# A projection weight read in quarters: its first piece in two halves, a small matrix requested later, and the first batch's input transposed at later steps

## The chip, the cores and the metric

The kernel runs on one NeuronCore of one Trainium2 chip. The metric is device time in microseconds (us): the median of several executions, each measured from start to end on the device. The engines of the core are TensorE (PE, matrix products; PEld is its weight load), VectorE (DVE), ScalarE (ACT), GpSimd (POOL) and SyncE (SP). SP and ACT also issue the DMA requests here; their queues are SPq and ACTq.

## The reference

Shapes: x is 8 batches of 512 tokens by 2048. A is 8 adapters of 2048x16 and B is 8 adapters of 16x2048 (the "cond" weights); W (`base_w`) is 2048x2048; `ffn_A` is 64x2048, `ffn_B` is 16 experts of 2048x64, `router_w` is 16x2048. Everything is float32.

```
cond    = (x @ B[id].T) @ A[id].T                     # rank 16, one adapter id for each batch
base    = cond @ W.T + base_b
hidden  = cond @ ffn_A.T                              # 64 wide
probs   = softmax(cond @ router_w.T)                  # 16 experts
combine = one_hot(top2(probs)) * (top2 / sum of top2)
delta   = sum over experts e of combine[e] * (hidden @ ffn_B[e].T)
out     = x + base + 0.5 * delta
```

## The kernel before, in words

Because cond has rank 16, the kernel never forms `cond @ W.T` for the tokens. It first builds G = W A for all 8 adapters (a 128x2048 matrix, 8 batches x 16 ranks by outputs). Then each batch needs only bx = B x (16 ranks by 512 tokens, spread over the partitions), the router on bx, and tile products of 128 tokens by 512 outputs.

**The setup stage** (up to the first tile of batch 0) reads W in 8 pieces of 256 rows (2 MB each, `load_w`, four requests of 512 KB, two from SP and two from ACT). The four buffers of `w_in` take turns. A piece gives 16 steps, so there are 128 steps `n` = 0 to 127: piece `g = n // 16`, slice `s = n % 16` of the contraction. In step n VectorE transposes a strided 128x256 slice of W into one of 8 places of a ring (`w_transpose(n)`, line 659, counted on semaphore `w_transposed`), and TensorE multiplies it with the gathered A (`w_product(n)`, line 866, two matmul rows in the trace for each product, counted on `w_used`). VectorE may be at most 8 steps ahead of TensorE, since `w_transpose(n)` waits until product n-8 is done.

Everything else of the setup is woven between these steps by tables of step numbers, written out by hand. All engines walk the same n, each at its own pace, and each executes its own list strictly in order:

- `BT_AT`: VectorE transposes B (`b_transposes`, line 665) after that step. `FA_AT`: it transposes ffn_A and router_w (line 647). `GLO_AT` = 40: at steps 40, 72 and 104 it splits a finished part of G (`take_g`, lines 695 and 701).
- `X_AT`: at which step VectorE transposes the j-th pair of slices of batch 0's x (line 728, from the buffer `xquad0`, four requests of 1 MB, line 290, two from each queue). There are 16 pairs. The tables `BX_AFTER` tell TensorE after which step it does the 16 products of the first and of the second half of x (line 941).
- `E_AT`: before which step TensorE flips expert group g (`expert_flips`, line 856, 8 transposes; written here as flips(g)). It waits for the group's load, `e_in`, written here as e0 to e15, requested by `load_experts` (line 250; steps in `E_LOAD_AT` on ACT, program order on SP). ACT copies the flipped group out (`copy_experts`, line 495, two activations 64x1024).
- `SLOT_AT`: the router chain of batch 0 in slots. Slot 8: ACT copies the finished bx products out of PSUM (`bxp`, the row `tmp<-ps`). Slot 9: TensorE forms the logits (line 949) and spreads bx (line 952), VectorE takes the row maximum (line 751) and subtracts it, ACT takes the exponential (line 554) and copies bx. Slot 10: VectorE finds the top two (lines 756 to 772). Slot 11: VectorE builds the combine matrix (lines 776 to 788). On VectorE a slot comes `SLOT_LAG` = 4 steps later than its table entry, on TensorE and ACT right at it. Inside one step n ACT runs its expert copy (`E_AT`) before its slot (`SLOT_AT`); TensorE runs the flips, the product, and then the slot.

The requests of SP and ACT go out in program order too. On ACT: token ids, A, W pieces 0 and 1, B, piece 2, the small matrices, e0, piece 3, e1, piece 4, e2, piece 5, e3, e4, x of batch 0, e5, piece 6, e6, e7, piece 7. SP's list is alike, with a small request for the bias rows (line 362) behind e1; e4 on both queues waits until these rows have landed (`s_biasrow`).

**The batch stage** then runs 8 batches of 16 tiles. Each tile is seven matmuls of 128x128 by 128x512 (lines 927 to 930), and one VectorE addition into the resident x (line 840).

Of the kernel before, what the change touches and what calls it, by code (L numbers as in the profile page):

```python
# [37 lines left out]
RING = 8  # L38
# [3 lines left out]
def adaln_ffn(nc, x, itok, cond_A, cond_B, base_w, base_b, ffn_A, ffn_B, router_w, out):  # L42
# [5 lines left out]
    KD = D // P  # L48
# [32 lines left out]
    with ExitStack() as ctx:  # L81
# [81 lines left out]
        s_load = [[sem(f"w_loaded{k}_half{h}") for k in range(WB)] for h in range(2)]  # L163
        s_ein = [sem(f"expert_in{k}") for k in range(7)]
# [44 lines left out]
        X_AT = {82 + 3 * j // 2: j for j in range(KD)}  # L209
        BX_AFTER = {90: 3, 101: 8}  # L210
        SLOT_AT = {103: 8, 106: 9, 109: 10, 112: 11, 115: 12, 119: 13, 123: 14}
        SLOT_LAG = 4
        GA_AFTER, SEL_AFTER = 42, 62
        BT_AT, FA_AT, GA_AT, SEL_AT = 24, 36, 56, 72
# [9 lines left out]
        WIDE_FROM = 2 * NT  # L224

# [65 lines left out]

        def load_w(eng, n, qs):

            need(eng, s_wt, (n - WB + 1) * KD)
            for q in qs:
                eng.dma_start(w_in[n % WB][q * SQ:(q + 1) * SQ], w_q[n, q]).then_inc(s_load[q // 2][n % WB], 16)  # L296
# [34 lines left out]
        def _(sp):  # L331
# [17 lines left out]
            load_w(sp, 0, (0, 1))  # L349
            sp.dma_start(bias_n[:, 0, :], base_b.rearrange("(a o) -> a o", a=BR)).then_inc(s_bias, 16)  # L350
            load_w(sp, 1, (0, 1))
            load_cond_b(sp, (0, 1))
# [4 lines left out]
            load_w(sp, 3, (0, 1))  # L357
            load_experts(sp, 1, 0)
# [134 lines left out]
        def _(act):  # L493
# [5 lines left out]
            load_w(act, 0, (2, 3))  # L499
            load_w(act, 1, (2, 3))  # L500
            load_cond_b(act, (2, 3))
# [4 lines left out]
            load_w(act, 3, (2, 3))  # L506
            load_experts(act, 1, 1)
# [5 lines left out]
            def copy_experts(g):  # L513

                act.wait_ge(s_ef, g + 1)
                for at, there, count in ((0, s_a, NB), (0, s_bT, KC), (1, s_fat, 2), (1, s_sm, 1),
                                         (2, s_xe, 2 * KD)):
                    if g == PER_C * at:
                        act.wait_ge(there, count)
                c, q, i = e_where(g)  # L520
                src = ps[:, e_bank(g):e_bank(g) + 2, :].rearrange("p b o -> p (b o)")\
                    .rearrange("p (a h m) -> p a m h", a=EG, h=2)
                dst = bexpT[q * R:(q + 1) * R, c, i * EG:(i + 1) * EG, :].rearrange("r a (m h l) -> r l a m h", h=2, l=2)
                for l in range(2):
                    ins = copy(dst[:, l], src[l * R:(l + 1) * R])
                ins.then_inc(s_ec, 1)
# [90 lines left out]
        def _(dve):  # L617
# [31 lines left out]
            def w_transpose(n):  # L649

                g, s = n // KD, n % KD
                if s == 0:
                    for half in range(2):
                        dve.wait_ge(s_load[half][g % WB], (g // WB + 1) * NQ // 2 * 16)
                need(dve, s_wmm, n - RING + 1)
                if n == 0:
                    dve.wait_ge(s_const, 1)
                src = w_in[g % WB].rearrange("p t (l r) -> p r t l", l=SQ)[:, s]
                dve.transpose(wT[:, n % RING, :].rearrange("p (t l) -> p t l", l=SQ), src).then_inc(s_wt, 1)  # L659

# [136 lines left out]
            take_a()  # L797
            for n in range(NW):
# [52 lines left out]
        def _(pe):  # L851
# [6 lines left out]
            def w_product(n):  # L858

                g, s = n // KD, n % KD  # L860
                if n == 0:
                    pe.wait_ge(s_a, NB)
                if s == 0:
                    need(pe, s_glo, g // 2 - 1)
                pe.wait_ge(s_wt, n + 1)
                pe.matmul(ps[:, ACC + g // 2 % 2, g % 2 * WN:(g % 2 + 1) * WN], a_t[:, s, :], wT[:, n % RING, :],  # L866
                          start=(s == 0), stop=(s == KD - 1)).then_inc(s_wmm, 1)

# [97 lines left out]
            first = Batch(0)  # L966
            for n in range(NW):
# [50 lines left out]
```

## Time and profile before

| | us |
|---|---|
| median of 3 runs | 446.18 |
| lowest, highest | 445.64, 464.56 |
| the profiled execution, whole | 445.62 |
| its span, first to last instruction | 443.8 |
| mean granted TensorE clock | 0.996 of full |

The profiled execution is the reference for all sums: its span is 443.8 us and 1.8 us lie around the span. Its whole time is 0.02 us under the lowest of the three runs; the highest run, 464.56 us, is far from the other two. The setup stage ends when the first tile's matmuls begin, 116.3 us after the span's start; the rest are the 8 batches.

### The profile page before, as it was taken

The page shows a single profiled execution, that of the slowest core. Times are in us where ns is not written, and L with a number is a line of the kernel's source. Part 1 is how long each engine was busy: PE and PEld are TensorE (multiplying, and loading weights), DVE is VectorE, ACT ScalarE, POOL GpSimd, SP SyncE. Part 2 cuts the span into 40 slices and gives each one's busy share as a digit, 9 for nine tenths or more (in the row PEclk, how much of TensorE's full clock was granted, in tenths as well). Part 3 has the DMA queues.
Part 4 walks back from the last instruction along what each step waited for, and adds up shares of the span by engine and source line. Part 5 has one row for each costly group of instructions (what it writes and reads, how often), then busy time and mean ns, then how long its engine had stood idle before and what let it go on. Part 6 is the DMA issues. An engine that isn't in the chain of part 4 may idle for free.

```text
span 443.8 us, 6785 instructions
## 1 busy us (share of the span) xinstructions
PE 409.7 (92%) x2496; PEld 279.9 (63%) x2496; DVE 319.4 (72%) x830; ACT 108.1 (24%) x163; POOL 40.5 (9%) x53
## 2 busy tenths in 40 slices
PE   0597997999788999999999999999999999999996
PEld 0475985656556766666667666666666676666665
DVE  2699996999468496668677875966686778756453
ACT  0003114435473231123113112311231131123110
POOL 4020000002100120012001201200120012012000
PEclk9999998999999999999999999999999999999999
DMA  8999999999999999899999999998999898556935
GB/s 223 357 330 331 334 357 366 345 269 336 289 295 239 352 362 323 279 349 342 310 287 378 306 315 302 366 312 295 348 335 325 285 366 303 207 201 217 343 128 189
DMA packets 75027, 135.35 MB, mean 305 GB/s; under 512 B 5506, under 2 KB 14770, under 8 KB 74994
## 3 DMA queue, kind: packets, MB, share of 16 engines
q1 hardware_dynamic: 56000, 102.08, 69.7%
q10 hardware_dynamic: 18994, 32.84, 23.5%
q8 instruction: 20, 0.33, 0.3%
q14 instruction: 13, 0.11, 0.1%
HBM read 99.23 MB, written 35.65 MB: 304 GB/s over the span
## 4 chain that ended last, share of the span: by engine, by line
PE 63%; DVE 10%; DMA 9%; SPq 6%; POOL 3%; ACT 3%; issue 3%; ACTq 2%; POOLq 0%; DVEq 0%
PE ps L927 13%; PE ps L928 11%; PE ps L929 11%; PE ps L901 11%; PE ps L941 6%; DMA bexpT<-in_x 6%; PE ps L930 5%; POOL u_r L480 3%; DMA gm_r<-xT 3%; DVE xT L728 3%; DVE early L659 3%; SPq L296 3%; ACT bexpT L495 2%; PE ps L856 2%; PE ps L949 2%
## 5 line engine op out<-in xcount | busy, mean ns | idle before, releaser
L840 DVE TENSOR_TENSOR xbuf<-ps,xbuf 128x512 f32<-128x512 f32 x128 | 86.7, 677 | 96.0 <-PE ps L930 96.0
L927 PE MATMUL ps<-h_r,u_r 128*128 128x512 f32 x256 | 108.8, 425 | 0.7
L928 PE MATMUL ps<-h_r,u_r 128*128 128x512 f32 x256 | 100.3, 392 | 0.0
L929 PE MATMUL ps<-h_r,u_r 128*128 128x512 f32 x256 | 100.1, 391 | 0.0
L866 PE MATMUL ps<-early 128*128 128x256 f32 x256 | 66.5, 408 | 22.6 <-DVE early L659 22.6
L728 DVE STREAM_TRANSPOSE xT<-xbuf 128x256 f32<-128x256 f32 x224 | 80.6, 410 | 0.0
L866 PEld LDWEIGHTS ps<-early 128*128 128x128 f32 x256 | 48.1, 201 | 36.8 <-issue 16.5
L927 PEld LDWEIGHTS ps<-h_r,u_r 128*128 128x128 f32 x256 | 48.1, 188 | 35.9 <-issue 16.7
L659 DVE STREAM_TRANSPOSE early<-xbuf 128x256 f32<-128x256 f32 x128 | 65.9, 577 | 5.3 <-issue 3.8
L901 PE MATMUL ps<-bexpT,cur 128*32 128x512 f32 x512 | 61.6, 598 | 2.2 <-DVE h_r L707 1.5
L495 ACT ACTIVATE h_r<-ps 128x512 fp32r<-128x512 f32 x64 | 36.2, 595 | 78.8 <-PE ps L901 78.4
L929 PEld LDWEIGHTS ps<-h_r,u_r 128*128 128x128 f32 x256 | 48.1, 188 | 10.9
L928 PEld LDWEIGHTS ps<-h_r,u_r 128*128 128x128 f32 x256 | 48.2, 188 | 9.8 <-issue 1.7
L930 PE MATMUL ps<-gm_r,sbx_r 128*128 128x512 f32 x128 | 50.1, 391 | 0.0
L495 ACT ACTIVATE bexpT<-ps 64x1024 f32<-64x1024 f32 x32 | 35.2, 1101 | 50.6 <-issue 21.5
L707 DVE TENSOR_TENSOR h_r<-ps,h_r 128x512 fp32r<-128x512 f32 x64 | 40.4, 671 | 3.7 <-ACT h_r L495 3.7
L901 PEld LDWEIGHTS ps<-bexpT,cur 128*32 128x32 f32 x512 | 13.5, 109 | 32.5 <-issue 30.3
L941 PE MATMUL ps<-xT,bT 128*32 128x256 f32 x512 | 33.3, 381 | 0.2 <-DVE xT L728 0.2
L473 POOL TENSOR_TENSOR sbx_r<-bx,sbx_r 32x512 fp32r<-32x512 f32 x8 | 10.4, 1297 | 241.2 <-ACT sbx_r L495 241.2
L941 PEld LDWEIGHTS ps<-xT,bT 128*32 128x32 f32 x512 | 17.3, 109 | 17.0 <-issue 5.1
L480 POOL TENSOR_TENSOR u_r<-tmp,u_r 128x512 fp32r<-128x512 f32 x16 | 20.6, 1287 | 74.1 <-ACT u_r L495 74.0
L930 PEld LDWEIGHTS ps<-gm_r,sbx_r 128*128 128x128 f32 x128 | 24.0, 188 | 5.2
(67 smaller groups left out, 205.3 us busy)
## 6 DMA issues: line engine op xcount, KB each, us to landing
out<-xbuf SPq DMA_DIRECT2D x31, 1024.0 KB, 7.3
xbuf<-in_x SPq DMA_DIRECT2D x28, 1024.0 KB, 7.4
xbuf<-in_x ACTq DMA_DIRECT2D x32, 512.0 KB, 10.9
xbuf<-in_x SPq DMA_DIRECT2D x32, 512.0 KB, 8.6
xbuf<-in_L_ffn_base_w SPq DMA_DIRECT2D x16, 512.0 KB, 19.3
xbuf<-in_L_ffn_base_w ACTq DMA_DIRECT2D x16, 512.0 KB, 20.1
gm_r<-g_hilo SPq DMA_DIRECT2D x128, 32.0 KB, 6.8
early_u<-in_L_ffn_B SPq DMA_DIRECT2D x10, 256.0 KB, 18.5
```

Source lines behind the costliest of these rows:

```text
L495: return act.activation(dst, src, ACT.Copy)
L659: dve.transpose(wT[:, n % RING, :].rearrange("p (t l) -> p t l", l=SQ), src).then_inc(s_wt, 1)
L707: dve.tensor_tensor(h_r[:, c % 2, 1, h, :], ps[:, HB + h, :], f32(h_r[:, c % 2, 0, h, :]), ALU.subtract).then_inc(s_hlo, 1)
L728: dve.transpose(xh[:, place, :].rearrange("p (t l) -> p t l", l=SQ), src).then_inc(s_xe, 1)
L840: dve.tensor_tensor(xs, ps[:, tile_bank(b.n, m), :], xs, ALU.add).then_inc(s_out, 1)
L866: pe.matmul(ps[:, ACC + g // 2 % 2, g % 2 * WN:(g % 2 + 1) * WN], a_t[:, s, :], wT[:, n % RING, :], start=(s == 0), stop=(s == KD - 1)).th ...
L901: ins = pe.matmul(ps[32 * j:32 * j + 32, HB + h, :], cur[:, b.q, 0:2 * RK], bexpT[:, c, 4 * h + j, :], start=True, stop=True)
L927: pe.matmul(acc, u_r[:, b.q, 0, h, tok_t], hi, start=(h == 0), stop=False)
L928: pe.matmul(acc, u_r[:, b.q, 0, h, tok_t], lo, start=False, stop=False)
L929: pe.matmul(acc, u_r[:, b.q, 1, h, tok_t], hi, start=False, stop=False)
L930: pe.matmul(acc, sbx_r[:, b.q, tok_t], gm_r[:, c * BANK:(c + 1) * BANK], start=False, stop=True)\
L941: pe.matmul(ps[at:at + BK, BXB, g * (T // 2):(g + 1) * (T // 2)], bT[:, j, f.half, :], xh[:, ring_place(f, j), :], start=(j < NQ), stop=(j ...
```

## The change

W's first piece is requested in two halves of 128 rows (each quarter request of 512 KB becomes two of 256 KB; the two first halves of each queue go out ahead of the second ones), with semaphores of its own. VectorE and TensorE go through the 16 slices with the first half (`first_transpose`, `first_product`, 128 wide), then again with the second half (the new branch for `n < KD` in `w_transpose` and `w_product`), and from step 16 on as before. B is requested behind W's piece 3 in place of behind piece 1, on both queues, and transposed after step 46 in place of 24. ffn_A goes from step 36 to 34. The 16 pairs of batch 0's x go from steps 82, 83, 85, ... 104 to steps 88, 89, 90, 91, 93, ... 106. `BX_AFTER` and `SLOT_AT` follow.

```diff
-        X_AT = {82 + 3 * j // 2: j for j in range(KD)}
-        BX_AFTER = {90: 3, 101: 8}
-        SLOT_AT = {103: 8, 106: 9, 109: 10, 112: 11, 115: 12, 119: 13, 123: 14}
+        X_AT = {88 + 5 * j // 4: j for j in range(KD)}
+        BX_AFTER = {94: 3, 104: 8}
+        SLOT_AT = {105: 8, 107: 9, 110: 10, 112: 11, 115: 12, 119: 13, 123: 14}
...
-        BT_AT, FA_AT, GA_AT, SEL_AT = 24, 36, 56, 72
+        BT_AT, FA_AT, GA_AT, SEL_AT = 46, 34, 56, 72
...
+        WT = WN // SQ // 2
...
+        def load_first_w(eng, qs):
+
+            for h in range(2):
+                for q in qs:
+                    eng.dma_start(w_in[0][q * SQ:(q + 1) * SQ, h * WT:(h + 1) * WT], w_q[0, q, :, h * WT:(h + 1) * WT])\
+                       .then_inc(s_w0[q // 2] if h == 0 else s_load[q // 2][0], 16)
...
             load_cond_a(sp, 0)
-            load_w(sp, 0, (0, 1))
+            load_first_w(sp, (0, 1))
             sp.dma_start(bias_n[:, 0, :], base_b.rearrange("(a o) -> a o", a=BR)).then_inc(s_bias, 16)
             load_w(sp, 1, (0, 1))
-            load_cond_b(sp, (0, 1))
             load_w(sp, 2, (0, 1))
             sp.wait_ge(s_const, 1)
             load_small(sp, (0, 1))
             load_experts(sp, 0, 0)
             load_w(sp, 3, (0, 1))
+            load_cond_b(sp, (0, 1))
             load_experts(sp, 1, 0)
...
                 act.wait_ge(s_ef, g + 1)
-                for at, there, count in ((0, s_a, NB), (0, s_bT, KC), (1, s_fat, 2), (1, s_sm, 1),
-                                         (2, s_xe, 2 * KD)):
-                    if g == PER_C * at:
+                for first, there, count in ((0, s_a, NB), (2, s_bT, KC), (PER_C, s_fat, 2), (PER_C, s_sm, 1),
+                                            (2 * PER_C, s_xe, 2 * KD)):
+                    if g == first:
                         act.wait_ge(there, count)
...
                 need(dve, s_wmm, n - RING + 1)
-                if n == 0:
-                    dve.wait_ge(s_const, 1)
+                if n < KD:
+                    wide = wT[:, n % RING, :].rearrange("p (h t l) -> p h t l", h=2, l=SQ)
+                    src = w_in[0][:, WT:2 * WT].rearrange("p t (l r) -> p r t l", l=SQ)[:, s]
+                    dve.transpose(wide[:, 1], src).then_inc(s_wt, 1)
+                    return
...
+            def first_transpose(s):
+
+                if s == 0:
+                    for half in range(2):
+                        dve.wait_ge(s_w0[half], NQ // 2 * 16)
+                    dve.wait_ge(s_const, 1)
+                need(dve, s_wmm0, s - RING + 1)
+                wide = wT[:, s % RING, :].rearrange("p (h t l) -> p h t l", h=2, l=SQ)
+                src = w_in[0][:, 0:WT].rearrange("p t (l r) -> p r t l", l=SQ)[:, s]
+                dve.transpose(wide[:, 0], src).then_inc(s_wt0, 1)
...
+                if n < KD:
+                    pe.wait_ge(s_wt, n + 1)
+                    pe.matmul(ps[:, ACC, WN // 2:WN], a_t[:, s, :], wT[:, n % RING, WN // 2:WN],
+                              start=(s == 0), stop=(s == KD - 1)).then_inc(s_wmm, 1)
+                    return
...
+            def first_product(s):
+
+                if s == 0:
+                    pe.wait_ge(s_a, NB)
+                pe.wait_ge(s_wt0, s + 1)
+                pe.matmul(ps[:, ACC, 0:WN // 2], a_t[:, s, :], wT[:, s % RING, 0:WN // 2],
+                          start=(s == 0), stop=(s == KD - 1)).then_inc(s_wmm0, 1)
```

How the tables move the instructions is seen best in the engines' own lists. The first place is TensorE from the product of step 82 on, where line 866 (895 after) is the W product, line 856 (882) the flips and line 941 (978) the products with x. Before:

```order
L866 MATMUL ps<-early 128x256 x6
L856 MATMUL ps<-ident,early_u 128x128 x8
L866 MATMUL ps<-early 128x256 x3
L941 MATMUL ps<-xT,bT 32x256 x16
L866 MATMUL ps<-early 128x256
L856 MATMUL ps<-ident,early_u 128x128 x8
```

The same place after:

```order
L895 MATMUL ps<-early 128x256 x6
L882 MATMUL ps<-ident,early_u 128x128 x8
L895 MATMUL ps<-early 128x256 x4
L882 MATMUL ps<-ident,early_u 128x128 x8
L895 MATMUL ps<-early 128x256 x3
L978 MATMUL ps<-xT,bT 32x256 x16
```

The flips before steps 88 and 92 keep their steps (they are expert groups 5 and 6); the first 16 products with x went from behind step 90, between the two flips, to behind step 94, after both.

The second place is VectorE from its last transposes of x to the maximum of the router (line 728, after 752: x; 659, after 672: W; 695 and 701, after 719 and 725: `take_g` of step 104; 751, after 775: the maximum in slot 9). Before:

```order
L728 STREAM_TRANSPOSE xT<-bexpT 128x256 x2
L695 CAST u_r<-ps 128x512
L701 TENSOR_TENSOR u_r<-ps,u_r 128x512
L659 STREAM_TRANSPOSE early<-xbuf 128x256 x6
L751 TENSOR_REDUCE mx<-ps 128x4
L753 TENSOR_TENSOR ex<-ps,mx 128x64
```

After:

```order
L719 CAST u_r<-ps 128x512
L725 TENSOR_TENSOR u_r<-ps,u_r 128x512
L672 STREAM_TRANSPOSE early<-xbuf 128x256
L752 STREAM_TRANSPOSE xT<-bexpT 128x256 x2
L672 STREAM_TRANSPOSE early<-xbuf 128x256
L752 STREAM_TRANSPOSE xT<-bexpT 128x256 x2
L672 STREAM_TRANSPOSE early<-xbuf 128x256 x5
L775 TENSOR_REDUCE mx<-ps 128x4
```

The last pair of x now stands behind `take_g`, with five transposes of W between it and the maximum, where `take_g` and six transposes stood.

The third place is ACT from the copy of bx out of PSUM (slot 8) to the copies of bx in slot 9; `bexpT<-ps` x2 is one expert copy. Before:

```order
L495 ACTIVATE tmp<-ps 128x512
L250 DMA bexpT<-in_L_ffn_B 64x4x256
L554 ACTIVATE ex<-ex 128x64
L495 ACTIVATE bx<-ps 128x512
L495 ACTIVATE sbx_r<-bx 64x512
L495 ACTIVATE bexpT<-ps 64x1024 x2
```

After:

```order
L505 ACTIVATE tmp<-ps 128x512
L253 DMA bexpT<-in_L_ffn_B 64x4x256
L505 ACTIVATE bexpT<-ps 64x1024 x2
L564 ACTIVATE ex<-ex 128x64
L505 ACTIVATE bx<-ps 128x512
L505 ACTIVATE sbx_r<-bx 64x512
```

The copy of expert group 8 went from behind slot 9 to ahead of its exponential, because slot 9 moved from step 106 to 107, the step of that copy.

## Rows read from the trace of the kernel before

**Rows 1.** The page, section 2: busy share of the DMA engines in 40 slices of 11.1 us.

```profile
DMA  8999999999999999899999999998999898556935
```

**Rows 2.** Waits of TensorE from 112 us on, the largest: total us, times, longest.

```profile
PE ps L856 <- ACT bexpT L495: 3.0, 4, 0.8
```

**Rows 3.** Timeline of VectorE, first 72 us: start us, us, instruction, count, idle before.

```profile
15.37 12.44 DVE L659 STREAM_TRANSPOSE early<-xbuf 128x256 f32<-128x256 f32 x25 [3.84 <-issue]
...
35.99 2.85 DVE L647 STREAM_TRANSPOSE bexpT<-bexpT 128x768 f32<-128x768 f32 x2
...
47.83 3.10 DVE L659 STREAM_TRANSPOSE early<-xbuf 128x256 f32<-128x256 f32 x6 [0.76 <-PE ps L866]
...
60.29 1.11 DVE L659 STREAM_TRANSPOSE early<-xbuf 128x256 f32<-128x256 f32 x2 [0.71 <-PE ps L866]
...
71.76 0.77 DVE L728 STREAM_TRANSPOSE xT<-bexpT 128x256 f32<-128x256 f32 x2 [3.49 <-DMA bexpT<-in_x]
```

**Rows 4.** ACT's two requests for W's first piece, and their landing.

```profile
L296 ACTq DMA_DIRECT2D xbuf<-in_L_ffn_base_w x2: 601/622/644, 2.0 to 2.7; - x2
DMA to landing us min/median/max: 10.5/11.5/12.6
```

**Rows 5.** The chain that ended last, its longest piece: start us, us, what.

```profile
47.18 24.46 DMA bexpT<-in_x
```

**Rows 6.** Timeline of VectorE, 85 to 98 us.

```profile
85.74 0.73 DVE L728 STREAM_TRANSPOSE xT<-bexpT 128x256 f32<-128x256 f32 x2
86.39 0.57 DVE L659 STREAM_TRANSPOSE early<-xbuf 128x256 f32<-128x256 f32 x1
86.88 0.73 DVE L728 STREAM_TRANSPOSE xT<-bexpT 128x256 f32<-128x256 f32 x2
...
93.11 0.66 DVE L695 CAST u_r<-ps 128x512 fp32r<-128x512 f32 x1
...
94.40 3.08 DVE L659 STREAM_TRANSPOSE early<-xbuf 128x256 f32<-128x256 f32 x6
...
97.54 0.23 DVE L751 TENSOR_REDUCE mx<-ps 128x4 f32<-128x64 f32 x1
```

**Rows 7.** SP's two requests for W's piece 6, and their landing.

```profile
L296 SPq DMA_DIRECT2D xbuf<-in_L_ffn_base_w x2: 2620/2918/3217, 56.9 to 60.2; - x2
DMA to landing us min/median/max: 19.3/19.5/19.7
```

**Rows 8.** SP's request for e5, and its landing.

```profile
L250 SPq DMA_DIRECT2D early_u<-in_L_ffn_B x1: 2247/2247/2247, 54.6 to 54.6; - x1
DMA to landing us min/median/max: 19.1/19.1/19.1
```

**Rows 9.** SP's request for e6, and its landing.

```profile
L250 SPq DMA_DIRECT2D early_u<-in_L_ffn_B x1: 2820/2820/2820, 62.8 to 62.8; - x1
DMA to landing us min/median/max: 18.2/18.2/18.2
```

**Rows 10.** Timeline of TensorE matmuls, 68 to 98 us.

```profile
73.07 3.76 PE L866 MATMUL ps<-early 128*128 128x256 f32 x8 [2.86 <-DVE early L659]
...
80.41 2.29 PE L941 MATMUL ps<-xT,bT 128*32 128x256 f32 x32
...
83.16 1.04 PE L856 MATMUL ps<-ident,early_u 128*128 128x128 f32 x8
84.03 2.75 PE L866 MATMUL ps<-early 128*128 128x256 f32 x12
...
92.92 0.94 PE L941 MATMUL ps<-xT,bT 128*32 128x256 f32 x4 [0.20 <-DVE xT L728]
```

**Rows 11.** Timeline of ACT and its queue, 93 to 101 us.

```profile
93.95 1.74 ACTq L250 DMA_DIRECT2D xT<-in_L_ffn_B  x2
95.78 0.60 ACT L495 ACTIVATE tmp<-ps 128x512 f32<-128x512 f32 x1 [4.93 <-issue]
...
99.66 1.07 ACT L495 ACTIVATE bexpT<-ps 64x1024 f32<-64x1024 f32 x1
```

**Rows 12.** Stretch 74 to 76 us: length, busy PE, PEld, DVE, ACT, POOL, granted clock, DMA share, GB/s.

```profile
74.00:76.00 2.00, 2.00 (x5) 1.32 (x5) 2.00 (x6) 1.31 (x2) 0.00 (x0) 0.50 1.06 366
```

More of the change, by code:

```diff
@@ L163, in adaln_ffn @@
         s_load = [[sem(f"w_loaded{k}_half{h}") for k in range(WB)] for h in range(2)]
+        s_w0 = [sem(f"w_first_half{h}") for h in range(2)]
+        s_wt0, s_wmm0 = sem("w_first_transposed"), sem("w_first_used")
         s_ein = [sem(f"expert_in{k}") for k in range(7)]
@@ L498, in _ @@
             load_cond_a(act, 1)
-            load_w(act, 0, (2, 3))
+            load_first_w(act, (2, 3))
             load_w(act, 1, (2, 3))
-            load_cond_b(act, (2, 3))
             load_w(act, 2, (2, 3))
@@ L506, in _ @@
             load_w(act, 3, (2, 3))
+            load_cond_b(act, (2, 3))
             load_experts(act, 1, 1)
@@ L797, in _ @@
             take_a()
+            for s in range(KD):
+                first_transpose(s)
             for n in range(NW):
@@ L860, in w_product @@
                 g, s = n // KD, n % KD
-                if n == 0:
-                    pe.wait_ge(s_a, NB)
+                if n < KD:
[3 more added lines that the diff above has]
+                    return
                 if s == 0:
@@ L966, in _ @@
             first = Batch(0)
+            for s in range(KD):
+                first_product(s)
             for n in range(NW):
```

## The prediction

> **What bounds the kernel now.** I read three things, in this order. First, from 112 us on TensorE is the engine that the rest wait for: its largest wait of the whole batch stage is 3.0 us in four pieces [rows 2]. So whatever the setup stage gains or loses reaches the end, and only the setup needs reading. Second, in the setup VectorE is the busy one. Its timeline shows nearly gapless transposes of W from 15.37 us, with these gaps: 3.84 us ahead of the first (W's first piece), 0.76 and 0.71 us where it had run 8 steps ahead of TensorE, and 3.49 us ahead of the first slice of x [rows 3]. Third, the DMA engines are full from the start, 8 or 9 tenths in every slice of the setup [rows 1]. The last quarter of batch 0's x was requested at 47.18 us and landed 24.46 us later, at 71.7 us: the longest piece of the chain of waits [rows 5]. So there are two limits one behind the other. Until 71.7 us it is the DMA stream, after it VectorE's own list, with 45 of 128 W steps and all 16 pairs of x still to do. What matters is how much work stands behind 71.7 us, and what can't be done ahead of it.
>
> **Part 1, the head start.** ACT's first 512 KB of W landed at 2.0 + 10.5 = 12.5 us, its second at 2.7 + 12.6 = 15.3 us, when VectorE began [rows 4]. The new first half is 512 KB on each queue, so VectorE starts near 12.6 us, 2.8 us earlier (it sat idle then, so this is free time). Against that stand 32 transposes of 128x128 in place of 16 of 128x256. A strided 128x256 one takes 0.49 us start to start (86.39 to 86.88 us) [rows 6], a strided 128x768 one 2.85 / 2 = 1.43 us [rows 3]: about proportional to size, little fixed cost. Half size is then 0.25 us at least. The upper bound is the contiguous 128x256 one, 0.65 / 2 = 0.33 us [rows 6]. I take 0.28, near the lower end because the two strided rows are nearest in kind: 32 x 0.28 - 16 x 0.49 = +1.1 us, bounds 0 and +2.8. TensorE's narrower products have no row; on TensorE they lie beside the transposes, and if they were slower than those, VectorE would start step 16 later by what bounds it, at most the same 2.8 us. Net: 1.7 us earlier, bounds 0 and 2.8.
>
> The Trainium skill, "DMA: Bandwidth & Descriptors", section "Bandwidth", speaks against the smaller requests: it wants DMAs of 1 MiB or more and gives 341 GB/s for 1 MB and 138 GB/s for 64 KB. Taken for single requests, an estimate from those figures: the first 1 MB would need up to 7.6 us in place of 3.1, the head start is gone and 1.7 us with it. By the row, the requests stand in full queues [rows 1], and I expect no such loss; the sum below would move by 1 us at most either way, since this part is covered.
>
> **Part 2, B later, ffn_A earlier.** The four B transposes and two of ffn_A are the same work at other steps: cost 0. 1 MB of B ahead of pieces 2 and 3 goes behind them, so they land earlier, and VectorE never waited for them. B now stands behind TensorE's long ffn_A products (after step 42), where VectorE lost 0.76 us, and gives TensorE time to catch up; I expect that gap and the 0.71 us one behind it to go [rows 3]. Bounds: 0 and 1.5 us. ACT's first expert copy no longer waits for B; it was not late because of it.
>
> **Part 3, x six steps later.** This is the term that counts. VectorE was ready for x at 71.76 - 3.49 = 68.27 us. Now: 68.27 - 1.7 (part 1) - 1.5 (part 2) + 6 x 0.49 (steps 83 to 88 ahead of x) = 68.0 us. With neither gain it would be 71.2. **Either way x, at 71.7 us, is later.** Nothing ahead of x's requests is added or taken away, only permuted, and the queues are full [rows 1], so I leave its landing where it is. Hence parts 1 and 2 save nothing by themselves: they only lengthen the wait for x, to some 3.7 us. What is saved is the six W steps that stood behind 71.7 us: 6 x 0.49 = 2.9 us.
>
> **What that triggers.** Walk on from 71.8 us: 16 pairs x 0.65 = 10.4, 18 W steps (89 to 106) x 0.49 = 8.8, `take_g` 94.40 - 93.11 = 1.3 [rows 6], 0.1 at the first: VectorE ends the last pair at 92.4 us. The same sum for before (22 W steps, no `take_g`) gives 93.1, as its row has it.
>
> (a) Slot 9. Before, the chain from the last pair to the router's maximum took 97.54 - 93.11 = 4.4 us: products with x, two requests on ACT (93.95, 1.74 us), ACT's copy (95.78) [rows 11], logits. VectorE didn't feel it, for `take_g` and six transposes ran until 94.40 + 3.08 = 97.48 us [rows 6]. After, only five transposes cover it, 2.5 us, so VectorE is ready at 94.9 and waits near 2 us: **a new wait in place of the old one**. Queued behind it: slot 9's subtraction, three W steps, then slot 10; ACT's exponential and TensorE's next W products wait for these.
>
> (b) TensorE is now earlier in its list than its data. Flips(5) stand before step 88, flips(6) before step 92. e5 lands at 54.6 + 19.1 = 73.7 us [rows 8], e6 at 62.8 + 18.2 = 81.0 [rows 9]. Step 92 is transposed by about 76.4 us (71.8 + 4 pairs + 4 steps), so TensorE stands from some 78 to 81 us. From 81.0: flips(6) 1.0, three W products (2.75 / 6 = 0.46 each) 1.4, first 16 x products 2.3, four 1.8, flips(7) 1.0, six 2.8, second 16 x products 2.3 [rows 10] = 93.6 us, against 92.4 + 0.75 = 93.15 by VectorE (0.75: before, the last of them ended at 92.92 + 0.94 = 93.86, and the last pair at 93.11). So slot 9 comes 0.4 us later: the maximum at 92.4 + 4.4 + 0.4 = 97.2 us. W's piece 6 lands at 60.2 + 19.7 = 79.9 [rows 7] and is needed for step 96 at 71.8 + 7 x 0.65 + 7 x 0.49 = 79.8: no wait worth counting.
>
> (c) ACT now copies group 8 (2 x 1.1 us) [rows 11] ahead of the exponential: bx copied by 96.1, copy until 98.3, exponential until 98.6; VectorE asks for it at 97.2 + 0.4 + 1.5 = 99.1. Covered by 0.5 us; without that cover each us is lost.
>
> **Sum.** At the maximum 97.54 - 97.2 = 0.3 us are left, and VectorE has one W step more behind it (112 in place of 111), 0.5 us. From slot 11 on both lists are equal. 2.9 saved, about 2.1 given back at slot 9: **0.8 to 0.9 us faster**. 445.62 - 0.9 = 444.7 for the profiled execution. That execution and the lower two of the three runs (445.64, 446.18) average 445.8; for a median I say 444.9 us.
>
> **Rivals.**
> *Landings earlier.* Piece 5 may now be requested up to 2 us earlier, since step 31 is done earlier. For it: x, piece 6 and e6 all come from the same stream, and VectorE would be ready 3.7 us ahead. Against it: the DMA engines have no free slice in which to be quicker [rows 1]. If all land 1 to 3 us earlier, that comes through whole: 442 to 444 us.
> *TensorE at half clock behind the new wait.* This is the one that ends slower. Before, 2.86 us of idle TensorE (70.2 to 73.07) [rows 10] was followed by a stretch at 0.50 granted clock, 1.2 in place of 2.4 GHz, with eight matmul rows in 3.76 us [rows 12, 10]. Now TensorE idles twice: near 69.5 to 73.7 us and near 78 to 81. The first costs nothing; its products are early. After the second the list is already 0.4 us late, so every us counts. If the clock falls there and stays low as long as before, 3.4 us of work at half speed costs 1.7 us on (b): maximum at 98.9, 1.4 us later than before, less 0.5: +0.9, 446.7 us. It decides from 0.9 us of extra delay on. For it: the same length of idle did it once. Against it: TensorE has worked for some us just ahead.
> The Trainium skill, "TensorE: Matmul & The Clock Gate", section "What's actually happening", says the same: idleness throttles, activity releases, and how many matmuls are slow differs from run to run. The trace agrees with the first (0.50 after the idle); the last would make the loss uneven between runs.
> *The head start counts after all* (x doesn't limit): part of the first rival, no other price.
> *x lands later*, by the extra requests at the start or another share between the queues: each us costs one, 446 us for one.
>
> **How the numbers follow.** Forecast 0.5 (444 to 446), landings earlier 0.2, half clock 0.2, x later or exponential uncovered 0.1. The range leaves out the far ends: 442.8 to 447.0 us. About 2% (8.9 us) is what a measurement of this kernel can tell from no change; all cases lie inside: faster 0.01, same 0.98, slower 0.01.
>
> **What would show it.** In the changed kernel: the first transpose near 12.6 us; a wait for x on VectorE of 2.5 to 4 us, ending at 71 to 72.5; a new wait of VectorE at the router's maximum, 1.5 to 2.5 us; TensorE waiting for expert loads near 73 and 81 us; first tile at 115.4 in place of 116.3 us. I am wrong if x lands before 70 us, if the wait at the maximum is missing, or if the batch stage (327.5 us from first tile to the end) changes by more than 0.5 us.

## The result

The changed kernel takes 448.15 us (median of 6 runs, 447.28 to 448.96), the kernel before 445.8 us (median of 6 runs, the highest at 464.56): ratio 1.0058, 95% interval 1.0039 to 1.0077. It is **2.4 us slower** (2.6 by the ratio), where 0.9 us faster was forecast, and lies above the range's end of 447.0. The profiled execution took 447.41 us with a span of 445.6 (before 445.62 and 443.8), so the two profiles differ by 1.8 us. Some executions of the kernel before and of several experiments, the profiled one of run 9 among them, lay 6 to 24 us above the others; ratios and the medians from here on leave them out, and run 9's profile isn't used.

VectorE in the setup, of the changed kernel (start us, us, instruction, count, idle before), to be laid beside [rows 3, 6]:

```profile
12.59 4.72 DVE L683 STREAM_TRANSPOSE early<-xbuf 128x128 f32<-128x128 f32 x16 [1.21 <-issue]
17.23 2.29 DVE L669 STREAM_TRANSPOSE early<-xbuf 128x128 f32<-128x128 f32 x8
19.91 2.34 DVE L669 STREAM_TRANSPOSE early<-xbuf 128x128 f32<-128x128 f32 x8 [0.39 <-PE ps L889]
...
57.84 1.11 DVE L672 STREAM_TRANSPOSE early<-xbuf 128x256 f32<-128x256 f32 x2 [0.18 <-PE ps L895]
...
69.77 0.77 DVE L752 STREAM_TRANSPOSE xT<-bexpT 128x256 f32<-128x256 f32 x2 [0.99 <-DMA bexpT<-in_x]
...
79.46 0.61 DVE L672 STREAM_TRANSPOSE early<-xbuf 128x256 f32<-128x256 f32 x1 [1.56 <-DMA xbuf<-in_L_ffn_base_w]
...
84.44 0.77 DVE L752 STREAM_TRANSPOSE xT<-bexpT 128x256 f32<-128x256 f32 x2 [2.74 <-PE ps L978]
...
95.01 2.53 DVE L672 STREAM_TRANSPOSE early<-xbuf 128x256 f32<-128x256 f32 x5
...
99.70 0.23 DVE L775 TENSOR_REDUCE mx<-ps 128x4 f32<-128x64 f32 x1 [2.15 <-PE ps L986]
```

The start at 12.6 us, the near end of the two old gaps behind TensorE, and the new wait at the maximum (2.15 us) are there as forecast. Two things are not. x came at 69.7 us, not 71.7, so its wait is 0.99 us. And at 84.44 us, at the ninth of the 16 pairs of x, stands **a wait of 2.74 us for TensorE that the forecast doesn't have**. VectorE ends the last pair at 95.0 us where 92.4 was forecast; the maximum follows at 99.70 (forecast 97.2, before 97.54).

TensorE's matmuls of the changed kernel, to be laid beside [rows 10]; L882 are the flips, L978 the products with x, L986 the logits, L964 the first product of a tile:

```profile
74.15 1.97 PE L882 MATMUL ps<-ident,early_u 128*128 128x128 f32 x8 [4.24 <-DMA early_u<-in_L_ffn_B]
...
81.46 1.09 PE L882 MATMUL ps<-ident,early_u 128*128 128x128 f32 x8 [1.93 <-DMA early_u<-in_L_ffn_B]
...
83.78 1.93 PE L978 MATMUL ps<-xT,bT 128*32 128x256 f32 x32
...
94.81 0.95 PE L978 MATMUL ps<-xT,bT 128*32 128x256 f32 x4 [0.20 <-DVE xT L752]
...
97.34 1.09 PE L882 MATMUL ps<-ident,early_u 128*128 128x128 f32 x8 [0.52 <-DMA early_u<-in_L_ffn_B]
...
98.70 0.96 PE L986 MATMUL ps<-cur,tmp 128*128 128x16 f32 x8
...
117.97 0.50 PE L964 MATMUL ps<-h_r,u_r 128*128 128x512 f32 x1
```

Flips(6) wait for e6 until 81.46; the first products with x stand behind them at 83.78. The transposes of x write into a ring of 16 places (`need(dve, s_bxq, ... k - KD + 1)`, two places a pair), so the ninth pair can't be written until the first of these products has read its place. The first tile is at 117.97 us, 1.65 later than before (116.32 us), and the remaining stage takes 327.6 us (before 327.5): all of the loss lies in the setup.

The chain of waits (start us, us, what) has x's piece 2 us earlier than in [rows 5], with the same length, and a new piece, the load of e8 (L318 is a request on SP's queue):

```profile
45.21 24.44 DMA bexpT<-in_x
...
76.12 0.92 SPq L318
77.08 20.21 DMA early_u<-in_L_ffn_B
97.34 1.09 PE ps L882 x8
```

The load e8 uses the buffer of e5, so its request can't go out before flips(5), which ended at 76.12 us here; SP's queue came to it at 77.08. In the kernel before, flips(5) ended at 78.56 us and the request followed at 78.59.

### The profile page after: what moved, and what is told of

It reads as the page before. It is cut to its first block, busy times and chain, and to the rows that moved or that the text cites. A ratio compares the mean times of both kernels' runs of the same rounds, so it can differ in the third digit from the quotient of the medians.

```text
span 445.6 us, 6871 instructions
## 1 busy us (share of the span) xinstructions
PE 410.9 (92%) x2528; PEld 281.9 (63%) x2528; DVE 321.0 (72%) x846; ACT 107.9 (24%) x163; POOL 40.4 (9%) x53
## 4 chain that ended last, share of the span: by engine, by line
PE 63%; DMA 14%; DVE 7%; SPq 6%; POOL 3%; ACT 3%; issue 3%; ACTq 1%; POOLq 0%; DVEq 0%
PE ps L964 13%; PE ps L965 11%; PE ps L966 11%; PE ps L938 11%; PE ps L978 6%; DMA bexpT<-in_x 5%; PE ps L967 5%; DMA early_u<-in_L_ffn_B 5%; DMA gm_r<-xT 4%; POOL u_r L490 3%; PE ps L882 2%; ACT bexpT L505 2%; SPq L306 2%; DVE xT L752 2%; PE ps L989 1%
## 5 line engine op out<-in xcount | busy, mean ns | idle before, releaser
L964 PE MATMUL ps<-h_r,u_r 128*128 128x512 f32 x256 | 108.8, 425 | 0.8
L964 PEld LDWEIGHTS ps<-h_r,u_r 128*128 128x128 f32 x256 | 48.0, 188 | 35.9 <-issue 16.7
L895 PE MATMUL ps<-early 128*128 128x256 f32 x224 | 56.7, 399 | 3.2 <-DVE early L672 3.2
L672 DVE STREAM_TRANSPOSE early<-xbuf 128x256 f32<-128x256 f32 x112 | 58.0, 575 | 1.7 <-DMA xbuf<-in_L_ffn_base_w 1.6
L895 PEld LDWEIGHTS ps<-early 128*128 128x128 f32 x224 | 39.8, 195 | 16.1 <-DVE early L672 11.4
L978 PE MATMUL ps<-xT,bT 128*32 128x256 f32 x512 | 33.1, 381 | 0.9 <-DVE xT L752 0.9
L978 PEld LDWEIGHTS ps<-xT,bT 128*32 128x32 f32 x512 | 17.2, 110 | 17.6 <-issue 5.1
```

The costliest lines, as they stand in the source:

```text
L964: pe.matmul(acc, u_r[:, b.q, 0, h, tok_t], hi, start=(h == 0), stop=False)
L978: pe.matmul(ps[at:at + BK, BXB, g * (T // 2):(g + 1) * (T // 2)], bT[:, j, f.half, :], xh[:, ring_place(f, j), :], start=(j < NQ), stop=(j ...
```

## The experiments

Run 1 is the label e1 and so on; e5, e6 and e8 without the word run are the loads of the experts' pieces.

All times of a row are of its profiled execution: us from the span's start to the maximum of slot 9 and to the first product of the first tile.

| kernel | median us | ratio to before, 95% | maximum | first tile |
|---|---|---|---|---|
| before | 445.1, 445.9, 445.9 (beside runs 1 to 4, 5 to 8, 9 to 12) | | 97.54 | 116.32 |
| changed | 448.15 | 1.0058 [1.0039, 1.0077] | 99.70 | 117.97 |
| run 1, x products first | 449.11 | 1.0084 [1.0057, 1.0112] | 100.85 | 119.71 |
| run 2, logits first | 450.95 | 1.0129 [1.0086, 1.0172] | 101.87 | 121.28 |
| run 3, both | 445.64 | 1.0009 [0.9974, 1.0044] | 96.13 | 115.81 |
| run 4, old step tables | 444.99 | 0.9994 [0.9968, 1.0020] | 96.06 | 115.91 |
| run 5, tables alone | 447.91 | 1.0052 [1.0031, 1.0074] | 100.07 | 118.38 |
| run 6, late B alone | 446.00 | 0.9996 [0.9978, 1.0014] | 97.53 | 116.31 |
| run 7, halves alone | 445.33 | 0.9990 [0.9964, 1.0015] | 95.39 | 114.18 |
| run 8, added matmuls | 447.95 | 1.0051 [1.0032, 1.0070] | 100.16 | 118.46 |
| run 10, all, reordered | 445.21 | 0.9985 [0.9962, 1.0008] | 96.34 | 115.47 |
| run 11, slot 10 later | 446.52 | 1.0013 [0.9991, 1.0036] | 95.18 | 116.30 |
| run 12, halves again | 444.57 | 0.9961 [0.9927, 0.9994] | 95.56 | 117.26 |

(Run 9 is told below.)

### Run 1 to run 4: which of the orders costs the time

Against the changed kernel, run 1 puts the first 16 products with x ahead of flips(6), run 2 the logits of slot 9 ahead of flips(8), run 3 both; run 4 takes all three step tables from the kernel before.

```
run 1, run 3:  -BX_AFTER = {94: 3, 104: 8}          +BX_AFTER = {91: 3, 104: 8}
run 2, run 3:  -SLOT_AT = {105: 8, 107: 9, ...}     +SLOT_AT = {105: 8, 106: 9, ...}
run 4:      X_AT, BX_AFTER and SLOT_AT as before; halves and late B stay
```

> The changed kernel with its first 16 products of x behind step 91 in place of 94, so ahead of the flips of expert group 6. Main theory (ring of x): VectorE's ninth pair of x waits for TensorE's first x product, which stood behind the flips that wait for e6. Then VectorE's wait of 2.7 us at 84.4 us goes, and its last pair of x ends near 92.3 us in place of 95.0. The router's maximum still waits for the logits behind the flips of group 8 (e8 lands at 97.3 us), so the time itself falls by only 0 to 0.6 us, to about 447.5. Rival (half clock of TensorE after its idle stretch): the wait stays within 0.5 us of 2.7, the time within 0.3 us. Rival (cost of the halves): nothing changes.

> The changed kernel with slot 9 at step 106 in place of 107, so the logits stand ahead of the flips of group 8 and the exponential ahead of ACT's copy of group 8. Main theory: the maximum is then held by ACT's copy of the x products alone (98.1 us), 0.7 us earlier than the changed kernel's 99.7: time 0.5 to 0.8 us less, about 447.3. Rival (the order at slot 9 is harmless, all comes from the x ring or the clock): no change within 0.2 us.

> Both edits: x products behind step 91, slot 9 at step 106. Main theory (two queue orders on TensorE, each behind an expert load): last pair of x at 92.3 us, maximum near 96.8 us in place of 99.7, time 2.7 to 3.0 us below the changed kernel and 0.5 to 1 below the kernel before, about 445.1. Rival (half clock): the two edits together bring less than 1 us, since TensorE stays slow. Rival (the halves cost): less than 1 us.

> The halves of W's first piece and the late B, with the x, product and slot tables of the kernel before. Main theory: the head start does count, because x lands 2 us earlier with it (69.7 us); TensorE meets the loads e5 and e6 as late in its list as before. Everything behind x moves 2 us ahead: about 443.8 us, faster than before by 2. My prediction's theory (x's landing fixed at 71.7 us, parts 1 and 2 covered) says 445.8, no change. Rival (the halves or the late B are what costs): 447 to 448, as the changed kernel.

Run 1 removed the wait of the ninth pair: VectorE ended the last pair at 91.2 us in place of 95.0. Against my expectation the time didn't fall. In its profile the first tile is 1.7 us later than in the changed kernel's; by the ratios (1.0084 and 1.0058, intervals that overlap) "slower" isn't shown. In the profile of run 1, TensorE and VectorE:

```profile
96.81 1.63 PE L882 MATMUL ps<-ident,early_u 128*128 128x128 f32 x8 [3.77 <-DMA early_u<-in_L_ffn_B]
...
99.08 1.73 PE L986 MATMUL ps<-cur,tmp 128*128 128x16 f32 x8
```

```profile
100.85 0.23 DVE L775 TENSOR_REDUCE mx<-ps 128x4 f32<-128x64 f32 x1 [7.10 <-PE ps L986]
```

```profile
97.00:99.00 2.00, 2.00 (x10) 1.90 (x10) 0.00 (x0) 0.53 (x1) 0.00 (x0) 0.55 1.05 168
99.00:101.00 2.00, 2.00 (x10) 1.92 (x9) 0.15 (x1) 1.61 (x2) 0.00 (x0) 0.50 1.09 280
```

(The last fence is a table by stretch: length, busy PE, PEld, DVE, ACT, POOL, granted clock, DMA share, GB/s.) VectorE was early, but the logits stand behind flips(8), and these behind e8, which landed at 96.8 us here (97.3 in the changed kernel) although VectorE was 3.8 us ahead. TensorE idled 3.77 us for it and then worked at half clock (0.55 and 0.50), so the maximum came 1.15 us later still. I call such an order, in which work that is ready stands behind flips that wait for a load, a lock. There are **two locks, one behind the other**: flips(6) ahead of the first products with x, and flips(8) ahead of the logits.

Run 2 opens only the second and leaves the first. Neither of my two expectations held: it is slower than the changed kernel, with intervals that don't overlap, and its setup ended later than in any other. In its profile the ninth pair waited 4.70 us, until 87.08. Little of that is due to the load: e6 came at 81.96 us, 0.5 us later than in the changed kernel. But TensorE had idled 4.83 us for it, and from the start of flips(6) to the first product with x it then took 4.45 us at a granted clock of 0.50, where the changed kernel took 2.32 us at 1.00. Run 2's edit moves nothing ahead of 95 us, so why the clock came out so there is open.

Run 3 opens both. Its maximum is 1.4 us ahead of before, and its wait of the ninth pair is gone. By its ratio (1.0009) it ends where the kernel before does; the 0.5 to 1 us less that I had expected isn't seen, and its interval doesn't exclude it.

In run 4, too, the maximum is 1.5 us ahead of before and the time the same (0.9994); the 2 us that I expected didn't come. The loss thus goes with the step tables, and a cost of the halves or of the late B isn't seen. Of the 1.5 us, one instruction of VectorE took 1.1 back (last section).

Run 3 and run 4 can't be told apart, so these runs show no gain from the six steps that x moved, even in a good order: run 3 waits less for x (2.57 us against 4.88), but waits 2.25 us at the maximum, where run 4 doesn't wait. The chain from the last pair of x to the maximum is what remains.

### Run 5 to run 7: each part alone, on the kernel before

```
run 5: -X_AT = {82 + 3 * j // 2: ...}   +X_AT = {88 + 5 * j // 4: ...}
       -BX_AFTER = {90: 3, 101: 8}      +BX_AFTER = {94: 3, 104: 8}
       -SLOT_AT = {103: 8, 106: 9, 109: 10, ...}  +SLOT_AT = {105: 8, 107: 9, 110: 10, ...}
run 6: -BT_AT, FA_AT, ... = 24, 36, ...   +BT_AT, FA_AT, ... = 46, 34, ...
       load_cond_b behind load_w(sp, 3, ...) and load_w(act, 3, ...), as in the change
run 7: -load_w(sp, 0, (0, 1))            +load_first_w(sp, (0, 1))       (ACT alike)
       +first_transpose(s), +first_product(s) for s in range(KD), as in the change
```

> The kernel before with the three step tables of the change alone (x at the later steps, its products and the slots at theirs); W's first piece stays whole, B stays behind W's first piece as it was. Theory (the ring of x places): the ninth pair of x transposes stands behind the first 16 x products, and these behind the flips that wait for e6; so VectorE shows a wait of 2 to 4 us for TensorE in the x transposes of steps 88 to 92, slot 9 a wait of about 2 us for the logits, and the time is 1.5 to 2.5 us over the kernel before, some 447.3. Rival (the loss comes from the halves or the late B): no such wait, 445.8 or less.

> The kernel before with B's request behind W's fourth piece and the request of A's part earlier, as in the change; W's first piece whole, old step tables. Theory (the order of the requests moves x's landing): x lands near 70.5 instead of 71.8, the max of slot 9 comes up to 1 us earlier, the time is 0 to 0.7 us under the kernel before. Rival (x lands earlier because of the halves): x lands at 71.7 and the time is that of the kernel before within 0.2 us.

> The kernel before with W's first piece in two halves of 128 rows and their 128-wide transposes and products; B at its old place, old step tables. Theory (x's landing is moved by the order of the requests, not by the halves): x lands at 71.5 to 72, the head start of about 1.7 us ends in a longer wait for x (about 5 us), and the time is that of the kernel before within 0.3 us. Rival (the halves bring x earlier): x lands near 70.5 and the max of slot 9 is 1 us earlier.

**The tables alone are the whole loss**: 1.0052 against 1.0058 of the full change, with the interval clear of 1. In the profile of run 5, TensorE and VectorE show the first lock and the wait at the maximum:

```profile
80.67 1.09 PE L856 MATMUL ps<-ident,early_u 128*128 128x128 f32 x8 [3.56 <-DMA early_u<-in_L_ffn_B]
...
83.97 2.59 PE L941 MATMUL ps<-xT,bT 128*32 128x256 f32 x32
...
98.96 1.06 PE L949 MATMUL ps<-cur,tmp 128*128 128x16 f32 x8 [0.22 <-ACT tmp L495]
```

```profile
85.06 0.77 DVE L728 STREAM_TRANSPOSE xT<-bexpT 128x256 f32<-128x256 f32 x2 [3.38 <-PE ps L941]
...
100.07 0.23 DVE L751 TENSOR_REDUCE mx<-ps 128x4 f32<-128x64 f32 x1 [1.88 <-PE ps L949]
```

The second lock cost nothing here: flips(8) didn't wait, and the logits waited for ACT's copy. The first cost more than its load: from flips(6) to the first product with x it took 3.30 us at a clock of 0.70, against 2.32 us at 1.00 in the changed kernel.

Late B alone changes nothing (x again at 71.69). Where its expectation speaks of "the request of A's part", the edit moves ffn_A's transposes. The halves alone are where x comes earlier, at 69.61 us: my expectation that the order of the requests does this fell, and its rival stands. In eight of the nine kernels with halves whose profile shows a wait for x, x came 1 us or more ahead of 71.69; in run 2 it came at 71.52. With old tables that comes through as a maximum 2.15 us ahead of before, with no wait there. Its median says less (0.9990): see run 12.

### Run 8: does the half clock cost anything in the changed kernel?

```
+for _ in range({88: 4, 92: 2}.get(n, 0)):      # ahead of the flips of steps 88 and 92
+    pe.matmul(ps[:, BXB, :], ident[:, :], a_t[:, 0:4, :]..., start=True, stop=True)
```

> The kernel after with six matmuls (128x128 by 128x512) added on TensorE, four ahead of the flips of step 88 and two ahead of those of step 92, into a bank that is written again before it is read, so that TensorE idles for about 2 us less there. Theory (the ring and the order of slot 9 cost the time, the clock does not): the time stays at 448 within 0.5 us, at a granted clock that no longer falls to half near 74. Rival (the half clock behind the wait for e5 costs it): the time falls by 1 us or more.

In the changed kernel and in run 8 the stretch 74 to 76 us reads:

```profile
74.00:76.00 2.00, 1.85 (x9) 1.85 (x10) 2.00 (x5) 0.78 (x1) 0.00 (x0) 0.50 1.07 316
```

```profile
74.00:76.00 2.00, 2.00 (x14) 1.87 (x14) 2.00 (x7) 1.96 (x3) 0.00 (x0) 1.00 1.06 348
```

The clock stayed at full speed there, and the time is that of the changed kernel (447.95 against 448.15 us): VectorE waited for the ring until 85.37 us all the same. But this isn't a clean test, since the slow stretch didn't go, it moved behind the wait for e6:

```profile
81.03 1.97 PE L882 MATMUL ps<-ident,early_u 128*128 128x128 f32 x8 [2.64 <-DMA early_u<-in_L_ffn_B]
82.79 1.99 PE L895 MATMUL ps<-early 128*128 128x256 f32 x6
84.72 1.93 PE L978 MATMUL ps<-xT,bT 128*32 128x256 f32 x32
```

From flips(6) to the first product with x it took 3.69 us at a clock of 0.61, so this product came 0.94 us later than in the changed kernel, although e6 came 0.43 us earlier. That the clock near 74 us costs nothing is seen better in the changed kernel's own trace: behind its slow stretch TensorE still waited 1.93 us for e6. A slow stretch ahead of that wait is free, one behind it is paid in full. By the profiles it lay ahead of it in the changed kernel and behind it in runs 2, 5 and 8. Whether other executions of the changed kernel had it behind, which would fit their spread from 447.28 to 448.96 us, no trace shows.

### Run 9 to run 12: can the idle time be used, and what spreads the runs?

```
run 9, on run 7:   +X_AT = {84 + 4 * j // 3: j ...}  +BX_AFTER = {91: 3, 102: 8}
run 10, on run 7:  +X_AT = {88 + 5 * j // 4: j ...}  +BX_AFTER = {91: 3, 104: 8}
                   -E_AT = {..., 107: 8, ...}        +E_AT = {..., 109: 8, ...}
                   +SLOT_AT = {105: 8, 108: 9, 111: 10, 113: 11, 116: 12, 119: 13, 123: 14}
run 11, on run 4:  +SLOT_AT = {103: 8, 106: 9, 112: 10, 114: 11, 116: 12, 119: 13, 123: 14}
run 12:            run 7, unchanged
```

> W's first piece in halves, B at its old place, and only a small part of the change's delay of x: x transposes at steps 84 to 104 (before 82 to 104, in the change 88 to 106), their products behind steps 91 and 102, slots at the old steps. Theory (VectorE's idle time for x is worth something only where x products, flips and logits keep their old order on TensorE): two W transposes move ahead of the wait, the wait for x shrinks by 1 us against the halves alone, no wait for TensorE appears in the x transposes or at the max of slot 9, and the time is about 1 us under the halves alone (some 444.3). Rival (the chain last x pair, product, copy, logits is already as long as VectorE's work beside it): the idle microsecond comes back ahead of the max and the time is that of the halves alone.

> W's first piece in halves, B at its old place, x at the change's late steps, but the products of x ahead of the flips that wait for e6, slot 9 at step 108 and the flips that wait for e8 behind it (step 109); slots 8, 10, 11 and 12 at steps 105, 111, 113 and 116. Theory: all of the wait for x but 2 to 2.5 us is gone, no wait in the ninth pair, the max of slot 9 waits under 1 us because two more W transposes stand ahead of it, and the first tile is 1 to 2 us earlier than with both orders restored and slot 9 at step 106: some 444. Rival (the chain from the last x pair to the max is what bounds, or the later slots make VectorE wait later): a wait of 1 us or more stands ahead of the max or of slots 13 and 14, and the time is 445.5 or more.

> The kernel with halves and late B on the old step tables, with slot 10 at step 112 instead of 109 and slots 11 and 12 at 114 and 116. Theory (the 1.34 us of VectorE's TENSOR_TENSOR beside GpSimd's is time in which VectorE waits for GpSimd's to end): with slot 10 three transposes later its TENSOR_TENSOR starts after GpSimd's has ended and takes 0.22 to 0.24 us, and the first tile is up to 1 us earlier than 115.9. Rival (it is that instruction's own cost in that kernel, or the next bound is the chain through slots 10 to 12): it takes over 1 us again, or it takes 0.22 us and the time doesn't fall.

> The kernel with the halves alone once more, unchanged, beside the kernels of this call. Its span was 441.8 us in one profile, with x at 69.6 and VectorE's TENSOR_TENSOR of slot 10 0.02 us ahead of GpSimd's; its median was 445.3. Theory (x's landing, which ended between 69.5 and 71.7 in the profiles so far, and who of the two engines starts first make its spread of 3 us): in this profile the first tile again follows from the two: 114.3 with x at 69.6, up to 2 us later with x at 71.7, and 1.1 us more if VectorE's instruction is stretched.

Run 9 (445.37 us, ratio 0.9989 [0.9958, 1.0021]) and run 10 are not distinguishable from the halves alone. For run 9 that is all that is known. In run 10 VectorE didn't wait for x at all, and waited 1.55 us for W's piece 6, 1.38 us at the maximum and 1.52 us near 110 us instead. These are the waits that its rival named, though the time of 445.21 us lies between the two expectations (some 444, and 445.5 or more). Time taken from one wait reappears in the next.

Run 12 is the most informative, because its expectation failed. x came at 69.79 us and VectorE's instruction wasn't stretched, so the first tile was to come near 114.5 us; it came at 117.26. Its maximum is only 0.17 us later than run 7's, but its first tile 3.08 us later. TensorE in the profile of run 7, then of run 12:

```profile
96.50 1.09 PE L882 MATMUL ps<-ident,early_u 128*128 128x128 f32 x8 [0.20 <-DMA early_u<-in_L_ffn_B]
```

```profile
98.53 1.97 PE L882 MATMUL ps<-ident,early_u 128*128 128x128 f32 x8 [2.06 <-DMA early_u<-in_L_ffn_B]
100.30 4.62 PE L895 MATMUL ps<-early 128*128 128x256 f32 x18
```

The stretch 98 to 100 us and VectorE, in run 12:

```profile
98.00:100.00 2.00, 1.47 (x7) 1.47 (x8) 1.71 (x15) 0.00 (x0) 1.24 (x1) 0.51 1.04 196
```

```profile
101.39 1.16 DVE L672 STREAM_TRANSPOSE early<-xbuf 128x256 f32<-128x256 f32 x2 [1.31 <-PE ps L895]
```

The load e8 landed 2 us later (98.5 against 96.5 us). Flips(8) waited, the granted clock behind that idle was 0.51, and VectorE, eight W steps ahead, had to wait 1.31 us. So once VectorE is early, the landing of e8 is the next bound. Of the 2 us, 1.2 are the request. In run 7 SP's queue issued it at 76.54 us, right behind flips(5), which ended at 76.51. In run 12 flips(5) ended at 76.61, but SP was busy with the request ahead of it until 77.66 and issued it at 77.70. The rest is the time to landing (19.9 and 20.8 us). e8 thus varies by about as much as the gain. This would explain why the halves alone are worth 2.15 us in one profile and 0.9990 [0.9964, 1.0015] and 0.9961 [0.9927, 0.9994] in two sets of runs: 0.4 us by the first, 1.7 by the second (which rests on 4 executions), and only the second interval leaves out 1. For the executions without a profile it isn't shown.

## Why the prediction was wrong

**What bounds the kernel: right.** TensorE waits in the batch stage are the same, its length is 327.5 to 327.6 us in both kernels, and the shifts of the setup came through whole in all profiles (327.5 to 327.7 us behind the first tile).

**Part 1, the head start: right in its start, a little short in size, wrong in its effect.** The start is at 12.59 us, and 32 transposes took 4.72 + 2.29 + 2.34 = 9.35 us, 0.29 each, where 0.28 was taken; between them VectorE waited 0.39 us for TensorE's narrower products. Step 16 began at 22.17 us, where before it began near 15.37 + 16 x 0.49 = 23.2: 1.0 to 1.1 us earlier, not 1.7. With part 2, VectorE was ready for x at 69.77 - 0.99 = 68.8 us, where 68.0 was forecast. The two first requests of each queue, 256 KB each, brought their 512 KB by 12.59 us, as the one request of 512 KB did before (12.5 us). The loss that the forecast estimated from the figures of the Trainium skill ("DMA: Bandwidth & Descriptors", "Bandwidth"), read as for single requests, isn't seen: by it the head start would have been gone. But "I leave its landing where it is" failed: x landed at 69.5 to 71.5 us in the nine profiles of kernels with halves that show a wait for it (run 9 left out), at 71.7 and 71.8 in the two without. By my own words a landing before 70 us makes the prediction wrong; here it cost nothing (below). In the kernel before, ACT's queue ends issuing x at 52.5 us and x lands at 71.6; in the changed one 50.6 and 69.7: about 19.1 us in both. Why that issue ends sooner I didn't settle.

**Part 2: right.** The gap of 0.76 us is gone, that of 0.71 is 0.18: 1.3 us, where 1.5 was counted. Alone (run 6) it is worth nothing.

**Part 3 and (b): this is the step that failed.** "Walk on from 71.8 us" counted pairs and steps on VectorE without asking what each pair needs. The ring has 16 places. In the kernel before, the first 16 products stood ahead of the flips that wait for e6; the change put them behind (94 in place of 90, flips(6) at 92). Sentence (b) itself had the number: flips(6) from 81.0, 1.0 us of flips, 1.4 us of W products, so first products at 83.4 us (measured 83.78). The walk had VectorE at the ninth pair at 71.8 + 8 x 0.65 + 10 x 0.49 = 81.9 us. The walk put this wait at nothing. By the prediction's own 83.4, and the 0.66 us from the first product to the ninth pair in the trace, the pair starts at 84.1 us, so the missing term is 2.2 us; by the measured 84.44 it is 2.5. With it, the forecast would have been 446.9 to 447.2 us for the profiled execution, which took 447.41. It swallows everything ahead of it: x 2 us earlier, the wait of 1.56 us for piece 6, the head start. Run 5, without halves and with x later, has its ninth pair at 85.06, 1.0 us of it by the slow clock.

**(a) slot 9: right in size, in part by luck.** 4.8 us were forecast from the last pair to the maximum; it is 99.70 - 95.01 = 4.69, with the wait (2.15) in the size named. But 0.4 of the 4.8 stood for TensorE being late in its own list (b), and it wasn't: its last product with x ended at 95.76, 0.75 us behind the last pair, as before. In its place stand flips(8), which the order had also put ahead of the logits and which waited for e8. ACT's copy, the last thing that the forecast counted ahead of the logits, ended at 98.07 us:

```profile
97.47 0.60 ACT L505 ACTIVATE tmp<-ps 128x512 f32<-128x512 f32 x1 [6.69 <-issue]
```

The logits began 0.63 us later, at 98.70 (before, 0.06 us later). Run 1 shows that this second lock, with the slow clock behind its wait, holds the maximum near 100 us even when VectorE is early. Had only the first lock been counted and opened, the forecast would have been wrong again.

**(c): right.** The exponential ended at 100.77 us and VectorE asked for it at 101.63. From the maximum to the first tile it is 18.3 us, 0.5 less than before (18.8), as the sum says.

**The rivals.** *Half clock behind the new wait* gave 446.7 us, the nearest number, but in the profile of the changed kernel not by its mechanism: the clock fell behind the first idle (for e5), where it is free, and was at 1.00 behind the second. In runs 2, 5 and 8 it did fall behind the second, as this rival says, and cost 2.1, 1.0 and 1.4 us there (against the 2.32 us of the changed kernel from flips(6) to the first product with x), on top of the lock; it did so behind the wait for e8 in runs 1 and 12. The Trainium skill ("TensorE: Matmul & The Clock Gate", "What's actually happening") says that idleness throttles. The rows agree in the changed kernel, run 1 and run 12 (4.24, 3.77 and 2.06 us of idle, then 0.50 to 0.55), but in run 3 the clock stayed at 1.00 behind 3.44 us of idle, so the length of one wait doesn't tell it. And it costs nothing until someone waits behind the slow stretch. *Landings earlier* happened for x and was worth nothing there, for the same reason.

## What to carry to other kernels

When a step is moved, walk every wait of the moved instruction, the ring it writes into too, and give each engine's walk the other's times: here both numbers (81.9 and 83.4 us) stood in the text and were never laid side by side. A consumer that is moved past an instruction that waits for a load inherits that load's landing, and so does the producer through the ring. Undo such orders together: one lock opened alone gained nothing here (runs 1 and 2), since TensorE then waits at the other, and the clock can fall behind that wait.

## What the hardware showed that I hadn't expected

**VectorE's small TENSOR_TENSOR can wait a whole GpSimd instruction.** In the profile of run 4, on VectorE and then on GpSimd:

```profile
98.38 1.34 DVE L784 TENSOR_TENSOR ex<-ex,rs 128x64 f32<-128x64 f32 x1
```

```profile
98.37 1.26 POOL L483 TENSOR_TENSOR sbx_r<-bx,sbx_r 32x512 fp32r<-32x512 f32 x1 [38.80 <-ACT sbx_r L505]
```

VectorE's takes 0.22 or 0.23 us in all profiles but this one and run 2's. Here GpSimd's had started 0.01 us earlier, and VectorE's ended 0.09 us behind it. In run 7 VectorE's starts at 97.73 us, GpSimd's at 97.75, and it is the other way round: 0.22 and 1.33 us.

```profile
97.73 0.22 DVE L784 TENSOR_TENSOR ex<-ex,rs 128x64 f32<-128x64 f32 x1
```

```profile
97.75 1.33 POOL L483 TENSOR_TENSOR sbx_r<-bx,sbx_r 32x512 fp32r<-32x512 f32 x1 [37.78 <-ACT sbx_r L505]
```

In run 2 one that started 0.50 us behind GpSimd's took 0.85 us. With slot 10 later (run 11) it started at 100.05 us, behind GpSimd's 97.49 + 1.27, and took 0.23 us, as its expectation said. That kernel was not faster, as its rival said: VectorE waited 0.95 us for TensorE behind flips(8), and 1.51 us near 111 us where run 4 waited 0.85. So a whole microsecond of this instruction hangs on 0.01 to 0.02 us between two chains. The Trainium skill, "SBUF — State Buffer", "SBUF: two separate sides", has the rule: whichever starts first, a VectorE operation with two SBUF inputs or a GpSimd operation that reads SBUF, holds their shared ports for its whole length. The rows of runs 4 and 2 agree, with VectorE's ending 0.09 and 0.08 us behind GpSimd's. The other way round it is less clear: GpSimd's took 1.33 us in place of 1.26, 0.07 more, where VectorE's had 0.20 us left.
